# A fused two-part transformer layer on one core: linear-attention state two steps ahead, column sums carried by a shifted n1, ny on ScalarE

## The reference, cut to what matters

```python
mod = (silu(c) @ wmod).reshape(16, 6, 1, -1)           # sa, ca, ga, sb, cb, gb
h = _layernorm(x) * (1 + ca) + sa                      # "n1", then "hT"
Q, K = elu(h @ Wq + bq) + 1, elu(h @ Wk + bk) + 1      # 16 heads of 8
KV, Ksum = einsum('nshd,nshm->nhmd', K, V), K.sum(axis=1)   # V = h @ Wv + bv
att = (Q KV) / (Q Ksum + 1e-6)
y1 = layer_norm(h + att @ Wo + bo, g1, beta1)          # "ny", then "x1T"
y2 = layer_norm(y1 + relu(y1 @ W1 + b1) @ W2 + b2, g2, beta2)    # "z"
x = x + ga * y2                                        # "x2"
h2 = _layernorm(x) * (1 + cb) + sb                     # "n3"
# token shift: every product below mixes a token with the one before it
r, k = sigmoid(mix_r(h2) @ Wr.T), square(relu(mix_k(h2) @ Wk.T))
out = x + gb * r * (k @ Wv.T)
```

## Time and profile before

| what | value |
|---|---|
| median of 3 runs | 173.39 us (173.34 to 176.28) |
| the profiled execution, its own time | 173.09 us |
| its span, first to last instruction | 171.4 us |
| granted PE clock, mean | 1.000 |
| PE, DVE, ACT, POOL busy | 94%, 80%, 63%, 62% of the span |

### The profile page before, as it was taken

How to read it: one execution, slowest core, us unless ns; L and a number is a source line. 1 busy time by engine, 2 the same in 40 slices (tenths; PEclk the granted TensorE clock), 3 DMA queues, 4 the chain that set the end, 5 groups by cost and what they waited for, 6 DMA issues and landing times. The chain is left out here.

```text
span 171.4 us, 4095 instructions
## 1 busy us (share of the span) xinstructions
PE 160.8 (94%) x1181; PEld 148.7 (87%) x1181; DVE 137.3 (80%) x618; ACT 107.3 (63%) x294; POOL 106.8 (62%) x235
## 2 busy tenths in 40 slices
PE   7995899999999999999989999999999999998883
PEld 7784689889999999999979999999999999787672
DVE  3644885989797979889896979797989788777852
ACT  3152573839393949586774949493939495737552
POOL 5233435575677777767695868676777756683531
PEclk9999999999999999999999999999999999999999
DMA  4529929900010101000010101010101010010012
GB/s 134 193 57 345 306 69 299 399 11 4 2 34 0 31 0 33 4 12 22 0 33 0 33 4 33 0 34 0 33 0 34 0 32 4 2 31 25 6 34 61
DMA packets 8347, 10.08 MB, mean 59 GB/s; under 512 B 723, under 2 KB 6534, under 8 KB 8326
## 3 DMA queue, kind: packets, MB, share of 16 engines
q1 hardware_dynamic: 7856, 9.54, 17.6%
q10 hardware_dynamic: 438, 0.28, 0.6%
q0 software_dynamic: 32, 0.01, 0.0%
HBM read 7.69 MB, written 2.13 MB: 57 GB/s over the span
## 5 line engine op out<-in xcount | busy, mean ns | idle before, releaser
L943 PE MATMUL bank<-w,hid 128*128 128x128 f32 x240 | 31.4, 275 | 0.0
L284 ACT ACTIVATE hT<-bank,modT 128x256 f32<-128x256 f32 x16 | 9.0, 565 | 35.4 <-PE bank L932 35.4
L975 PE MATMUL bank<-x1T,w 128*128 128x256 f32 x120 | 30.9, 380 | 0.0
L943 PEld LDWEIGHTS bank<-w,hid 128*128 128x128 f32 x240 | 29.0, 192 | 0.0
L975 PEld LDWEIGHTS bank<-x1T,w 128*128 128x128 f32 x120 | 21.5, 190 | 2.5 <-ACT x1T L288 0.2
L432 POOL TENSOR_TENSOR rstd_n<-vare_n,power 128x2 f32<-128x2 f32 x30 | 21.3, 708 | 2.4
L430 POOL TENSOR_TENSOR vare_n<-mv_n,eps 128x2 f32<-128x2 f32 x30 | 6.0, 200 | 18.9 <-DVE mv_n L540 18.9
L546 DVE TENSOR_SCALAR ny<-bank,mv_ny,rstd_ny 128x128 f32<-128x128 f32 x32 | 11.7, 406 | 5.4 <-POOL rstd_ny L432 5.4
L276 ACT ACTIVATE keepT<-bank,modT 128x255 f32<-128x255 f32 x28 | 14.3, 563 | 0.6 <-PE bank L932 0.6
L531 DVE BATCH_NORM_STATS2 stats_z<-bank 128x6 f32<-128x128 f32 x30 | 7.4, 289 | 8.2 <-PE bank L943 8.1
L430 POOL TENSOR_TENSOR vare_z<-mv_z,eps 128x2 f32<-128x2 f32 x14 | 2.8, 197 | 17.9 <-DVE mv_z L540 17.9
(11 more groups left out here) (176 smaller groups left out, 480.1 us busy)
## 6 DMA issues: line engine op xcount, KB each, us to landing
gm_rows<-mod_rows_dram SPq DMA_DIRECT2D x2, 960.0 KB, 9.0
out<-out_sb SPq DMA_DIRECT2D x15, 128.0 KB, 1.8
gm_rows<-mod_rows_dram SPq DMA_DIRECT2D x1, 768.0 KB, 6.2
w<-in_w SPq DMA_DIRECT2D x1, 512.0 KB, 4.9
bv_row<-bv_rows_dram SPq DMA_DIRECT2D x1, 512.0 KB, 11.7
x_all<-in_x SPq DMA_DIRECT2D x1, 384.0 KB, 4.4
bv_row<-bv_rows_dram SPq DMA_DIRECT2D x1, 384.0 KB, 5.5
gm_rows<-mod_rows_dram SPq DMA_DIRECT2D x1, 384.0 KB, 4.7
```

The source lines that it names most:

```text
L943: last = nc.tensor.matmul(banks[6][:, c * D:(c + 1) * D], hid[:, f, c * 128:(c + 1) * 128], w2[:, f, :], start=False, stop=(f == FF - 1 an ...
L975: return nc.tensor.matmul(bank[:, f % 2 * L:(f % 2 + 1) * L], w1[:, f * 128:(f + 1) * 128], x1T[:, :], start=True, stop=True)
```

## The change

Samples keep their phases, but the distances differ and so do the lists:

- the loop runs over t = 4 to 17 with A at t, B at t-2, F at t-3, N at t-4, C at t-5; what belongs to samples 0 to 3 before that is a list of its own on each engine, and the last three samples are finished by h2 products (mixing by two weight sets) in a list of its own. Samples 0 and 1 get their V bias by two products (direct_rows) and not through DRAM.
- n1 is written as normalised x plus one: POOL computes std and mean minus std (first_scale: four operations in the place of two). n1 times k then holds the column sums of k in every row. The k_pair addition, the column product and POOL's two maskings go; the state product takes wv_plus (128 columns and 16 columns of 1/128, so 144), and DVE masks the result in one operation. POOL adds the bias row to wv_mod beforehand (plus_row).
- ny is written by ACT from the bank, with a scale and a shift. DVE writes minus_mean, POOL multiplies it by the reciprocal root (shift_ny). ACT has two operations per sample more.
- kvs, qT and x2 have three buffers, hT three, wv_mod two.

```diff
             def norm_scale(name, count):
...
+            def first_scale(s):
+                need(pool, mv_ok["n1"], s + 1)
+                nc.gpsimd.tensor_tensor(vare["n1"][:, :], mv["n1"][:, :, 1], eps[:, :], ALU.add).then_inc(vare_ok["n1"], 1)
+                need(pool, vare_ok["n1"], s)
+                nc.gpsimd.tensor_tensor(rstd["n1"][:, :], vare["n1"][:, :], power[:, :], ALU.pow).then_inc(rstd_ok["n1"], 1)
+                need(pool, rstd_ok["n1"], s)
+                nc.gpsimd.tensor_tensor(std_n1[:, :], vare["n1"][:, :], rstd["n1"][:, :], ALU.mult).then_inc(std_ok, 1)
+                need(pool, std_ok, s)
+                nc.gpsimd.tensor_tensor(mean_n1[:, :], mv["n1"][:, :, 0], std_n1[:, :], ALU.subtract).then_inc(mean_ok, 1)
+
+            def y_scale(s):
+                norm_scale("ny", s + 1)
+                need(pool, minus_ok, s + 1)
+                need(pool, rstd_ok["ny"], s + 1)
+                need(pool, ny_ok, s)
+                nc.gpsimd.tensor_tensor(shift_ny[:, :], minus_mean[:, :], rstd["ny"][:, :], ALU.mult).then_inc(shift_ny_ok, 1)
+
+            def plus_row(s):
+                need(pool, wvm_ok, s - 1)
+                need(pool, kv_mm, s - 1)
+                pool.wait_ge(bv_in[part_of(BV_PARTS, s)], 16)
+                nc.gpsimd.tensor_tensor(wv_plus[s % 2][:, 0:D], wv_mod[s % 2][:, :], bv_row[:, s, :], ALU.add).then_inc(wvp_ok, 1)
...
+            def take_ny(s):
+                need(act, x1T_mm, s)
+                need(act, shift_ny_ok, s + 1)
+                for c in range(NC):
+                    last = nc.scalar.activation(ny[:, c, :], banks[1][:, c * D:(c + 1) * D], ACT.Identity,
+                                                scale=rstd["ny"][:, c:c + 1], bias=shift_ny[:, c:c + 1])
+                last.then_inc(ny_ok, 1)
...
-                    nc.tensor.matmul(banks[3][:, D:D + 1], k_pair[:, :], ones[:, :], start=True, stop=True).then_inc(aks_mm, 1)
...
+            def state(s):
+                need(pe, a_ok, s + 1)
+                if s < DIRECT:
+                    pe.wait_ge(direct_ok, 2 * (s + 1))
+                else:
+                    need(pe, wvp_ok, s - 1)
+                nc.tensor.matmul(banks[3][:, 0:D + H], a_sb[:, :], wv_plus[s % 2][:, :], start=True, stop=True).then_inc(kv_mm, 1)
...
+            turn_ny(0)
+            read_state(1)
+            hidden_products(0)
+            turn_att(1)
+            feed_forward_out(0, 0, 2)
+            projection(1)
+            feed_forward_out(0, 2, FF)
+            turn_ny(1)
```

More of the change, by code:

```diff
@@ new lines, in keeps, with positive_kk @@
+            def keeps(s):
+                need(act, mix_ok, s)
+                need(act, h2T_mm, s + 1)
+                nc.scalar.activation(keepT[:, :, 0:1], modT[:, FIRST:FIRST + 2, s:s + 1], ACT.Copy)
+                for i in range(2):
+                    last = nc.scalar.activation(keepT[:, i, 1:L], banks[2][:, 0:L - 1], ACT.Identity, scale=mod_col(KEEP + i, s),
+                                                bias=mod_col(SB, s))
+                last.then_inc(keep_ok, 1)
+            def positive_kk(s):
+                need(act, kk_mm, s + 1)
+                nc.scalar.activation(relu_k[:, :], banks[0][:, 0:L], ACT.Relu).then_inc(reluk_ok, 1)
@@ new lines, in _ @@
+            exponent_q(2)
+            positive_q(2)
+            take_a(2)
+            take_hT(3)
+            exponent_k(3)
+            take_rows()
+            exponent_q(3)
+            positive_q(3)
+            take_a(3)
+            take_ny(0)
+            take_x1T(0)
+            act.wait_ge(b1_ok, 1)
+            hidden(0, 0)
+            hidden(0, 1)
+            take_attT(1)
+            hidden(0, 2)
+            hidden(0, 3)
+            modulate_wv(4)
+            modulate_wv(5)
@@ new lines, in turn_att, with projection @@
+            def turn_att(s):
+                need(pe, att_ok, s + 1)
+                need(pe, hT_ok, s + 3)
+                need(pe, reluk_ok, s - 3)
+                transpose_in(banks[0], att, attT_mm)
+            def projection(s):
+                need(pe, attT_ok, s + 1)
+                for c in range(NC):
+                    residual_into(banks[1], hT[s % 3], c)
+                    last = nc.tensor.matmul(banks[1][:, tokens(c)], attT[:, tokens(c)], wo, start=False, stop=(c == NC - 1))
+                last.then_inc(y_mm, 1)
@@ L941, in feed_forward_out, with hidden_products @@
+            def hidden_products(s):
+                for f in range(FF):
+                    hidden_product(s, f, (banks[7], banks[6])[f // 2])
+            def feed_forward_out(s, f0, f1):
+                if f0 == 0:
+                    need(pe, hidb_ok, s + 1)
+                    for c in range(NC):
+                        residual_into(banks[6], x1T, c)
                 for f in range(f0, f1):
                     for c in range(NC):
[L943 to L944 removed]
@@ new lines, in _ @@
+            turn_n1(0)
+            direct_rows()
+            bv_product()
+            key_of(0)
+            query_of(0)
+            turn_n1(1)
+            key_by_n1(0)
+            key_of(1)
+            state(0)
+            query_of(1)
+            turn_n1(2)
+            read_state(0)
+            key_by_n1(1)
+            second_modulation()
+            state(1)
+            key_of(2)
+            query_of(2)
+            turn_att(0)
+            key_by_n1(2)
+            projection(0)
```

1307 lines of the change are left out of this document (677 added, 630 removed).

## The result

The changed kernel takes **185.39 us** (median of 4 runs, 184.41 to 187.08) beside 173.45 for the kernel before on the same chip: a ratio of 1.0703, with a 95% interval of 1.0612 to 1.0793. The prediction was 177.0 with a range up to 180. The profiled execution has a span of 182.9 us and an own time of 184.6, so 7.7 us of span stand over the 175.2 that the prediction's sum gave.

What follows compares the result with a forecast made beforehand. PE's own work was taken to bound the full steps, dependent chains the end. Span 171.4 - 1.45 (head) - 2.4 (full steps) + 7.6 (end) = 175.2; with 1.69 outside and the median's offset, 177.0 us, range 173.3 to 180.

Steps and rivals of the forecast that it cites:

- A full step: Steps 5 to 15: without the column product and with a shorter key product, a step falls from 8.97 to 8.78 us.
- rival (4): Full steps: the saved 0.14 and 0.08 come back as PE waits for weights, giving 179.2 us; chance 0.07.
- Does PE stay full?: Full steps: ACT about 7.2, DVE about 7.4, POOL about even, all below 8.78, so PE sets the step.
- The bump: Step 9: POOL's mix weights at the end of step 8 make it longer by 0.85 us.
- Rival (2): Full steps: ACT holds the step; at 0.3 us a step over 13 steps, 180.9 us; chance 0.12.
- The head: Before step 5: it starts at 44.7 against 46.15, a term of -1.45, but owes 6.6 us of PE work.
- The two stalls: Head: PE waits 2.45 us before the turning of ny(1) and 1.5 before that of ny(2).
- The gain of 0.15 us: Chain to ny: a skill-page estimate that ACT writing ny from PSUM shortens it by some 0.15 us; not used.
- The end: From step 16 on: two steps of 8.4 us and 16.2 behind them, 33.1 against 25.46, a term of +7.6.
- a wait inside the full steps, which counts elevenfold: Full steps: named at the prediction's close as one thing that would make it wrong.

Runs made afterwards that it cites:

- c5: Changed kernel with POOL's x plus shift and output sum each computed for only two of 128 columns per chunk; 181.94 us.
- c9: Changed kernel with POOL's wide operations reordered, output sum waiting for n3, tail work spread over three steps; 180.44 us, ratio 1.0354.
- c7: Changed kernel with the head's modulation products before the bias products and two more idle products; 184.45 us, ratio 1.0667.
- c11: c9 plus the head's modulation products before the bias products, twelve idle products before turning ny(1), and ny back on DVE; 179.19 us.
- c4: Changed kernel with two more statistics per step on DVE, written to a tile nothing reads; 185.66 us.
- c6: Changed kernel with ny written by DVE again, as in the kernel before; 183.31 us, ratio 1.0599.

## Why the prediction was wrong

The direction was right, the size was less than a third of what came: 3.6 us were forecast, 11.9 measured. By its own steps:

- **"A full step", 8.78 us: right as PE's own length.** Step 5, the steps of c5 and those of c9 have 8.82 with PE busy throughout. That is 0.15 under the 8.97 of before, where 0.19 was forecast. The column product's 0.14 and the key product's 0.08 did not come back as waits: rival (4) is false.
- **"Does PE stay full?", where I took DVE from 7.88 "to about 7.4": this is the step that failed.** Two things were missing. The smaller: DVE's list in the new order is busy 8.26 to 8.29 us even without any collision (c5, c9). Aggregates stand right behind their statistics and att behind its reciprocal, and each such pair costs 0.1 to 0.2 us more: a pair of statistics takes 0.52 from its start to the next operation's when its own aggregate follows, 0.41 in the kernel before where another operation stands there. I had the pair's row and didn't add it up. The larger: I laid the four lists of a step under each other with fixed durations and looked for late inputs alone, never for two operations that slow each other. x2 +0.5 and qT +0.4 brought DVE's list to 8.82 busy and the step to 9.24, 0.42 over PE's length; with the two apart the same work takes 8.82 (c9). The full steps came out at 102.6 us for 97.4.
- **The bump, 0.85: came as 1.9 over PE's 8.82**, where POOL's work for the tail met a step without room (1.5 over the ordinary 9.25; 1.11 in the kernel before). Over 8.82 stand: six steps at 9.25 (2.6 in all), step 6 0.38, step 9 1.92, step 11 0.71, step 15 0.04. 11 x 8.82 + 5.6 = 102.6.
- **Rival (2), ScalarE holds the step at +0.3:** right in what one sees (steps over 9), false in the engine. ScalarE is busy for 7.3 of 9.24, and c5 and c9 leave its list as it is. The prediction gave it 0.12, and had no rival for DVE at all.
- **The head, 44.7 for step 5:** 45.95. The two stalls came as laid out (turn of ny(1) at 36.53 behind 2.25 us for 35.25 and 2.45; the relus' wait 1.26 for 1.4; ny(2) 0.87 for 1.5). What was missing lies before them: sample 0's hidden products start at 27.92 where 26.8 was laid out. In front stand 1.0 us for the weights of the bias products, which the new list puts first, and the low clock behind it; c7, without that wait, reads the state of sample 1 0.6 us earlier, and how the rest is shared out no run shows. The chain to ny was also misread by a little: from 18.8 to 21.54 are 2.7 us and not 2.9, and from projection(1) to the turn of ny(1) it measured 3.1 where 3.3 was laid out. The gain of 0.15 us that the prediction's estimate gave for ny on ACT does not show: ACT writes a chunk of ny from the bank in 454 ns, where DVE took 406.
- **The end, 33.1:** 34.3. Steps 16 and 17 took 8.83 and 8.46 for 8.4 each, the rest 17.0 for 16.2; 6.6 us of it is the work owed by the head, as the prediction says.

The PE waits of the changed kernel that stand for the last two points:

```profile
31.40 0.44 PE L1079 MATMUL bank<-ident,x1T 128*128 128x128 f32 x2 [1.26 <-ACT hid L331]
36.53 0.44 PE L1074 MATMUL bank<-ident,ny 128*128 128x128 f32 x2 [2.25 <-ACT ny L317]
45.45 0.44 PE L1074 MATMUL bank<-ident,ny 128*128 128x128 f32 x2 [0.87 <-ACT ny L317]
...
156.93 0.44 PE L1074 MATMUL bank<-ident,ny 128*128 128x128 f32 x2 [0.50 <-ACT ny L317]
161.06 0.33 PE L1079 MATMUL bank<-ident,hT 128*128 128x128 f32 x1 [0.76 <-ACT attT L311]
```

The line "a wait inside the full steps, which counts elevenfold" named the danger and gave it no engine and no chance. With the collisions gone (c9, and c11 with the head's changes) the run is 179.2 to 180.4, 1.2% to 1.9% over the forecast; what remains over the kernel before, some 3%, is the term of head and end that the prediction had, and the 1 us in front of it. None of the versions beats the kernel before. Whether two steps of lead can be had without paying for them in the end was not tried.

## What to carry to other kernels

When operations are moved, look at what stands beside them on the other engine and not at their order alone: an operation with two SBUF inputs on DVE that starts beside a running wide one on POOL takes up to twice its time, POOL's takes longer where DVE's came first, and one that reads PSUM takes what it always does. A busy PE of 100% can hold waits: compare the start-to-start time of the same records in two steps before calling PE the bound. And a probe that adds or removes work also shifts everything behind it; read the durations of the shifted operations before the total (c4 added 0.45 us at no cost, c6 added 0.56 and its period fell from 9.24 to 9.00).

## What the runs showed of the hardware that was not expected

- Beside a POOL addition of 128x256 with two SBUF inputs, qT (128x256, two SBUF inputs) takes 0.83 us in place of 0.41, n3 (two tensor_scalar of 128x128 from SBUF) 1.08 in place of 0.65, when POOL's began first; POOL's addition keeps its 0.73. When qT began first it keeps its 0.41, and POOL's takes 0.90 to 0.94. qT ends 0.28 behind POOL's operation wherever it started inside it. Statistics, and operations with one input in PSUM, keep theirs.
- TensorE starts every one of the fourteen traces at half cadence (0.21 us from one record of 128 columns to the next, 0.11 later). The trace has no clock record before the first rise, and a view that covers this stretch prints 1.00 for it. The rise lay at 4.7 us in one execution and at 13.7 in another, 12.5 and 5.3 with the same list up to there. Start-to-start times show it, the clock's column does not.
